# Sharing four score copies between ScalarE and VectorE, folding in one strided operation, and moving the first keys to another PSUM bank

## The chip, the cores and the metric

The kernel runs on one core of one Trainium2 chip. The metric is the device time of one execution in microseconds. It is a single launch, with all tensors in the chip's memory at the start and the output written there at the end.

## The reference

The input is x, 8 batches of 128 tokens with 512 channels, and a context of the same shape. Three blocks follow one another, each added to its input and followed by a layer norm:

```
x = layernorm(x + self_attention(x))      # 32 query heads, 8 key/value heads, 128 wide, 4-bit weights, causal mask
x = layernorm(x + cross_attention(x, ctx))
x = layernorm(x + expert_layer(x))        # dense product plus the two best of 8 low-rank experts
```

The change lies almost wholly in the second block, whose softmax runs over axis 0, which is the axis of batches and heads together:

```
Q, K, V = x @ Wq.T + bq, ctx @ Wk.T + bk, ctx @ Wv.T + bv       # 16 heads of 32 channels
Q, K, V = each as (8 batches * 16 heads) matrices of 128 tokens x 32
scores = einsum('bqd,bkd->bqk', Q, K) / sqrt(32)                  # b: 128 batch-head pairs
attn = softmax(scores, axis=0)                                    # over the 128 pairs, not over the keys
out = einsum('bqk,bkd->bqd', attn, V)
```

So for each query and each key position the largest of 128 scores, and the sum of 128 exponentials, are wanted: eight batches of sixteen heads.

## The kernel before

The program writes each engine's instruction stream by hand; engines meet only through semaphores, and each engine executes its own stream in order. PSUM has eight banks of 512 float32 columns, called banks[0] to banks[7].

**Self-attention** takes most of the time. It runs in phases; TensorE's `phase(f)` projects queries, keys and values for phase f + 1, computes scores and weighted values of phase f, and multiplies the finished heads of phase f - 1 with the output weights. The products rotate over banks 0, 1, 2 and 7 (`product_ps`). VectorE reads twelve of every sixteen output products out of PSUM (`add_out`, L1246); ScalarE reads the other four, those with u = 3, 7, 11, 15 (`scale_out`, L900), and GpSimd adds them (L711). `wait_out_read(eng, p, u)` waits until product u of part p has been read, on the semaphore of whichever engine reads it.

**The seam** between the blocks begins after the last `phase` call on TensorE (after the line `n = BPH * LAST` in TensorE's function). TensorE first waits for the keys' weights and the context, then for the read of output product 15 of part LAST - 2, and then computes the first four channels-by-token units of the cross-attention's keys (`keys(0..3)`, L1856, into `proj2_bank(i)`, banks[7]), interleaved with the last scores (L1622), transposes, weighted values and output products of self-attention. `out_bank` places the products of part LAST - 1 in banks 0, 1, 2 by u % 3. `turn_y` (L1810) transposes accumulated outputs back to token order, using banks 0, 1, 2 for the first four batches. The layer norm of the first four batches and the last sixteen output products (`outs_last`) follow, then the query units and the transposes of the other half.

**Cross-attention scores** are made a half at a time, four batches each: half 0 is batches 0 to 3, half 1 is batches 4 to 7. For one batch, `scores2(b)` (L1825) issues 16 matmuls into four whole banks, banks 0 to 3 for even b and 4 to 7 for odd b, so batch b needs batch b - 2 copied out. The matmuls go to 128 x 2048 results: 16 groups of 128 columns, a group being one head. `copy_scores2(b)` on ScalarE (L1069) moves all 2048 columns to the SBUF tile `xs[:, SLOT[b], :]` in one instruction and increments `scores2_copied`.

Around the scores, TensorE executes in this order: `scores2(0..3)`; a wait for three copies; eight units of 8 matmul instructions each for the other half's keys and queries (L1686); `scores2(4..7)`; a wait for seven copies; then `values(0..7)`, eight units for V (L1839, with a one-row matmul of the bias at L1835 ahead of the first three); and then `attend(b)` (L1941) and `turn_att(b)` (L1950) by batch.

VectorE computes, for each half h: `maximum2(h)`, three elementwise maxima over the four batches (L1431) and `fold`; `shift(h)`, subtracting the maximum from four batches (L1436), which releases ScalarE's exponentials (L1074) one by one; `add_exps(h)`, three elementwise sums (L1444) and `fold`. `fold` reduces 2048 columns, 16 groups of 128, to 128 columns in four halving operations (L1418 three times, L1419 once), each waiting for the one before through a semaphore. At the end of half 1 come the reciprocal and `weigh(b)` (L1463), one multiplication of 2048 columns for each batch, and `add_attended(b)` (L1469), which reads `turn_att`'s result.

After that follow the second layer norm, the expert layer and the output; the change does not touch them.

Of the kernel before, what the change touches and what calls it, by code (L numbers as in the profile page):

```python
# [14 lines left out]
AX = mybir.AxisListType  # L15

P = 128
NB = 8
T = NB * P
D = 512  # L20
KC = D // P
# [6 lines left out]
BPH = NB // 2  # L28
# [15 lines left out]
LN_GROUPS = [[(0, 2), (2, 2), (4, 2), (6, 2)], [(0, 2), (2, 2), (4, 2), (6, 2)], [(0, 2), (2, 2), (4, 2), (6, 1), (7, 1)]]  # L44
UNITS = 24
UNIT_ORDER = list(range(UNITS))
SLOT = [4, 5, 6, 7, 0, 1, 2, 3]
APART = 5
ROPE_TILES = [0, 2, 3, 4, 5]
# [4 lines left out]
OUTS = QPK * KC  # L54
RING = 3
LAST = 2 * NKV - 1
# [10 lines left out]
def wait(eng, sem, value):  # L67

    if isinstance(value, int) and value <= 0:
        return  # L70
    eng.wait_ge(sem, value)


def build(nc, t, out):
    with ExitStack() as ctx:
# [3 lines left out]
        def sem(name):  # L79
            return ctx.enter_context(nc.semaphore(name))  # L80
# [31 lines left out]
        def carve(*shape, base=None):  # L112
            n = int(np.prod(shape))
            if base is not None:
                at[0] = base
            a = at[0]
            at[0] += n
            assert at[0] <= ARENA, at[0]
            v = arena[:, a:a + n]
            if len(shape) == 2:  # L120
                return v.rearrange("p (a b) -> p a b", b=shape[1])
            if len(shape) == 3:
                return v.rearrange("p (a b c) -> p a b c", b=shape[1], c=shape[2])
            return v
# [93 lines left out]
        xs = carve(NB, XH * P, base=0)  # L218
# [68 lines left out]
        banks = [ps[:, i, :] for i in range(8)]  # L287
# [72 lines left out]
        proj2_copied = sem("proj2_copied")  # L360
        scored2 = sem("scored2")
        scores2_copied = sem("scores2_copied")
        shifted2 = sem("shifted2")
        apart2_ready = sem("apart2_ready")
        factor2_ready = sem("factor2_ready")
# [50 lines left out]
        def out_by_act(u):  # L416

            return u % KC == KC - 1

        def dve_index(u):  # L420
            return DVE_TILES * (u // KC) + u % KC

        def wait_out_read(eng, p, u):

            if out_by_act(u):
                wait(eng, out_scaled, KC * p + u // KC + 1)
            else:
                wait(eng, out_added, DVE_TILES * QPK * p + dve_index(u) + 1)
# [15 lines left out]
        def product_bank(name):  # L444
            return product_ps[PRODUCTS.index(name) % 4]
# [22 lines left out]
        def out_bank(p, u):  # L468

            if p == LAST - 1:  # L470
                return banks[u % 3]
            if p == LAST:
                return product_ps[u % 4]
            return product_bank(f"O{u}")
# [50 lines left out]

        def turn_y_bank(b):

            return banks[b % 3] if b < BPH else banks[5 + b % 2]

        def turn2_bank(layer, b):  # L530

# [4 lines left out]
        def proj2_bank(i):  # L536

            if i < KC:
                return banks[7]
            if i < 2 * KC:  # L540
                return banks[(3, 4, 0, 1)[i - KC]]
            return banks[i % 3]

        def scores2_banks(b):

            return ps[:, 4 * (b % 2):4 * (b % 2) + 4, :]
# [283 lines left out]
        def _(act):  # L830
# [79 lines left out]
            def copy_k2(i):  # L910

                n, half = i % KC, i // (2 * KC)
                act.wait_ge(proj2_done, UNIT_ORDER.index(i) + 1)
                nc.scalar.activation(k2_halves[half][:, n, :], proj2_bank(i), ACT.Identity,
# [145 lines left out]
            def copy_q2(i):  # L1060

                n, half = i % KC, i // (2 * KC + KC)
                act.wait_ge(proj2_done, UNIT_ORDER.index(i) + 1)
                nc.scalar.activation(q2_halves[half][:, n, :], proj2_bank(i), ACT.Identity,
                                     bias=bias_qk[:, n:n + 1]).then_inc(proj2_copied, 1)

            def copy_scores2(b):
                act.wait_ge(scored2, b + 1)
                nc.scalar.activation(xs[:, SLOT[b], :], scores2_banks(b).rearrange("p a n -> p (a n)"),  # L1069
                                     ACT.Copy).then_inc(scores2_copied, 1)  # L1070

            def exps2(b):
                act.wait_ge(shifted2, b + 1)
                nc.scalar.activation(xs[:, SLOT[b], :], xs[:, SLOT[b], :], ACT.Exp, scale=XSCALE).then_inc(exp2_done, 1)  # L1074

# [6 lines left out]
            def copy_v2(b):  # L1082

                i = 4 * KC + b
                act.wait_ge(proj2_done, UNIT_ORDER.index(i) + 1)
                nc.scalar.activation(v2[:, b, :], proj2_bank(i), ACT.Copy).then_inc(proj2_copied, 1)

            n = BPH * LAST
# [106 lines left out]
        def _(dve):  # L1195
# [174 lines left out]
            n = BPH * LAST  # L1370
# [31 lines left out]
            def step(ins):  # L1402

                nonlocal soft_steps
                soft_steps += 1
                ins.then_inc(soft_step, 1)
                dve.wait_ge(soft_step, soft_steps)
# [4 lines left out]
            def by_group(v):  # L1412
                return v.rearrange("p (g q) -> p g q", q=P)

            def fold(v, op, dst):

                for n in (1024, 512, 256):
                    step(nc.vector.tensor_tensor(v[:, 0:n], v[:, 0:n], v[:, n:2 * n], op))  # L1418
                step(nc.vector.tensor_tensor(dst, v[:, 0:P], v[:, P:2 * P], op))  # L1419

            def maximum2(h):

                for b in range(BPH * h + 1, BPH * (h + 1)):
                    maximum_with(h, b)
                fold(x_max, ALU.max, x_m[h])

            def maximum_with(h, b):

                first = BPH * h
                dve.wait_ge(scores2_copied, b + 1)  # L1430
                step(nc.vector.tensor_tensor(x_max, xs[:, SLOT[b], :], xs[:, SLOT[first], :] if b == first + 1 else x_max,  # L1431
                                             ALU.max))

            def shift(h, *tiles):
                for b in tiles or range(BPH * h, BPH * (h + 1)):
                    nc.vector.tensor_tensor(by_group(xs[:, SLOT[b], :]), by_group(xs[:, SLOT[b], :]), over_groups(x_m[h]),  # L1436
                                            ALU.subtract).then_inc(shifted2, 1)

            def add_exps(h):

                first = BPH * h
                for b in range(first + 1, first + BPH):
                    dve.wait_ge(exp2_done, b + 1)
                    step(nc.vector.tensor_tensor(x_sum, xs[:, SLOT[b], :], xs[:, SLOT[first], :] if b == first + 1 else x_sum,  # L1444
                                                 ALU.add))
# [16 lines left out]
            def weigh(b):  # L1462
                nc.vector.tensor_tensor(by_group(xs[:, SLOT[b], :]), by_group(xs[:, SLOT[b], :]), over_groups(x_r[b // BPH]),  # L1463
                                        ALU.mult).then_inc(weights2_ready, 1)
# [52 lines left out]
            for k in range(3):  # L1517
                products, tiles, count = first_products(k)
# [47 lines left out]
            for k in range(3):  # L1566
                products, tiles, count = first_products(k)
# [25 lines left out]
        def _(pe):  # L1593
# [68 lines left out]
            def project_out(p, u):  # L1662

                h, nt, half = u // KC, u % KC, p % 2
                if u == 0:
                    wait(pe, heads_ready, BPH * (p + 1))
                if nt == 0:
                    wait(pe, wo_ready, QPK * (p // 2) + h + 1)
                if p < LAST - 1:
                    wait_product_bank(p + 1, f"O{u}")  # L1670
                elif p == LAST - 1 and u >= 3:
                    wait_out_read(pe, p, u - 3)
                elif p == LAST:
                    wait(pe, proj2_copied, KC)
                    if u >= 4:
                        wait_out_read(pe, p, u - 4)
                for k, part in enumerate((heads_hi, heads_lo)):
                    mm = nc.tensor.matmul(out_bank(p, u), wo_sb[:, h, nt * P:(nt + 1) * P], part[:, half, h, :],  # L1678
                                          start=(k == 0), stop=(k == 1))
                mm.then_inc(out_done, 1)  # L1680
# [136 lines left out]

            def scores2(b):

                wait(pe, scores2_copied, b - 1)  # L1820
                half, tokens = b // BPH, slice((b % BPH) * P, (b % BPH + 1) * P)
                for n in range(KC):
                    for i in range(4):
                        rows = slice(XD * i, XD * i + XD)
                        mm = nc.tensor.matmul(scores2_banks(b)[:, i, n * P:(n + 1) * P], k2_halves[half][rows, n, tokens],  # L1825
                                              q2_halves[half][rows, n, tokens], start=True, stop=True)
                mm.then_inc(scored2, 1)
# [33 lines left out]
            n = BPH * LAST  # L1861
            pe.wait_ge(k2_in, 16)
            pe.wait_ge(ctx_in, 16 * 2 * KC)
            wait_out_read(pe, LAST - 2, OUTS - 1)
            keys(0, 0, 1, 2, 3)
            scores(n)
            scores(n + 1)
# [45 lines left out]
            pe.wait_ge(proj2_copied, 2 * KC)  # L1913
            for b in range(BPH):
                scores2(b)
            pe.wait_ge(scores2_copied, BPH - 1)
            for i in range(8, 12):
                wait(pe, proj2_copied, i - 2)
                channels_by_token(i, wk2, ctx_t[:, :, HALF:])
# [6 lines left out]
            pe.wait_ge(proj2_copied, 4 * KC)  # L1926
            for b in range(BPH):
                scores2(BPH + b)
            pe.wait_ge(scores2_copied, NB - 1)
            for b in range(NB):  # L1930
                values(b)

# [193 lines left out]
```

## Time and profile before

| what | value |
|---|---|
| median of 3 runs | 675.29 us (674.85 to 675.7) |
| the profiled execution's own time | 674.36 us |
| its span | 672.6 us |
| PE busy | 633.9 us, 94% |
| DVE busy | 547.4 us, 81% |
| ACT busy | 452.0 us, 67% |
| POOL busy | 407.0 us, 61% |
| granted TensorE clock, mean | 0.995 |

The span leaves 1.76 us of the profiled execution's time outside it. PE is TensorE's matmuls, PEld its weight loads, DVE is VectorE, ACT is ScalarE, POOL is GpSimd. A busy share is an average over stages that have different limits, so the stages are read one by one: the timeline gives the instructions of all engines in order of time with the idle time ahead of each and who ended it; the chain of waits follows the work that ended last backwards from the last instruction, and is shown in order of time; the windows view gives the busy time of each engine in a stretch and the granted clock.

### The profile page before, as it was taken

How to read it: one execution, taken by the hardware profiler on the slowest of the kernel's cores; microseconds unless marked ns; L12 is line 12 of the kernel's file. 1: busy time of each engine (PE TensorE's matmuls, PEld its weight loads, DVE VectorE, ACT ScalarE, POOL GpSimd, SP SyncE). 2: the span in 40 equal slices, each digit the busy share in tenths (PEclk: the TensorE clock that was granted, in tenths of full speed). 3: DMA queues.
4: the chain of work that ended last, by engine and by line, in shares of the span. 5: the costliest groups of instructions: out<-in, count | busy, mean ns of one | idle time of the engine just before them, and what ended most of it. 6: DMA issues, size and time to landing. Idle time of an engine off the chain costs nothing. (4 is left out here: it accounts for less than half of the span.)

```text
span 672.6 us, 11232 instructions
## 1 busy us (share of the span) xinstructions
PE 633.9 (94%) x3358; PEld 443.2 (66%) x3358; DVE 547.4 (81%) x944; ACT 452.0 (67%) x1293; POOL 407.0 (61%) x351
## 2 busy tenths in 40 slices
PE   8889999999999999999999999999998989978996
PEld 4557787777878778687777877856554444447552
DVE  5977898998989889899898998975462968998357
ACT  6598787969869788796976978776644545622100
POOL 1576899899799889989979888791240000012003
PEclk9999999999999999999999999999999998999998
DMA  7864532534442252153244223330010000020003
GB/s 237 260 167 117 165 94 67 164 86 108 120 132 48 79 164 56 36 165 83 64 116 121 57 55 104 106 105 18 0 64 1 0 1 1 0 98 2 1 0 125
DMA packets 30189, 57.00 MB, mean 85 GB/s; under 512 B 4784, under 2 KB 5040, under 8 KB 29616
## 3 DMA queue, kind: packets, MB, share of 16 engines
q1 hardware_dynamic: 30128, 56.28, 29.0%
q8 instruction: 27, 0.44, 0.3%
q14 instruction: 34, 0.28, 0.1%
HBM read 33.19 MB, written 2.10 MB: 52 GB/s over the span
## 5 line engine op out<-in xcount | busy, mean ns | idle before, releaser
L1216 DVE SCALAR_TENSOR_TENSOR arena<-ps,scales,arena 128x512 f32<-128x512 f32 x288 | 212.5, 745 | 27.2 <-PE ps L1604 11.2
L1604 PE MATMUL ps<-x_hi,w_sb 128*128 128x512 f32 x384 | 164.6, 429 | 8.3 <-DVE y L1246 3.4
L1246 DVE SCALAR_TENSOR_TENSOR y<-ps,out_scales,y 128x512 f32<-128x512 f32 x192 | 139.2, 744 | 16.9 <-PE ps L1678 16.6
L1604 PE MATMUL ps<-x_lo,w_sb 128*128 128x512 f32 x384 | 151.9, 396 | 0.0
L686 POOL TENSOR_TENSOR arena<-arena,consts 128x512 f32<-128x512 f32 x75 | 96.7, 1289 | 21.5 <-DVE arena L1216 20.4
L859 ACT ACTIVATE arena<-ps,small 128x128 f32<-128x128 f32 (+1 forms) x256 | 84.4, 360 | 36.6 <-DVE small L1224 31.2
L1678 PE MATMUL ps<-heads_hi,wo_sb 128*128 128x512 f32 x256 | 108.8, 425 | 0.1
L692 POOL TENSOR_TENSOR arena<-arena,consts 128x512 f32<-128x512 f32 x75 | 96.9, 1292 | 16.1 <-DMA arena<-arena 15.4
L711 POOL TENSOR_TENSOR y<-arena,y 128x512 f32<-128x512 f32 x64 | 82.5, 1289 | 32.5 <-ACT arena L900 30.5
L1604 PEld LDWEIGHTS ps<-x_hi,w_sb 128*128 128x128 f32 x384 | 72.8, 190 | 42.8 <-DVE arena L1216 10.7
L1678 PE MATMUL ps<-heads_lo,wo_sb 128*128 128x512 f32 x256 | 101.0, 394 | 0.0
L809 POOL TENSOR_SCALAR var_eps<-mean_var 128x2 f32<-128x2 f32 (+1 forms) x13 | 7.0, 542 | 154.7 <-DVE mean_var L1354 154.7
L702 POOL TENSOR_TENSOR arena<-arena 128x512 f32<-128x512 f32 x75 | 96.8, 1291 | 5.6
L850 ACT ACTIVATE arena<-ps,scales 128x512 f32<-128x512 f32 x96 | 67.3, 701 | 22.3 <-PE ps L1604 21.9
L1604 PEld LDWEIGHTS ps<-x_lo,w_sb 128*128 128x128 f32 x384 | 73.1, 190 | 10.2
L877 ACT ACTIVATE arena<-arena,small 128x128 f32<-128x128 f32 (+1 forms) x256 | 76.4, 400 | 0.0
L1622 PEld LDWEIGHTS ps<-arena 128*128 128x128 f32 x512 | 66.3, 191 | 8.0 <-issue 3.5
L1622 PE MATMUL ps<-arena 128*128 128x128 f32 (+1 forms) x512 | 64.3, 269 | 0.8 <-POOL arena L702 0.4
L1678 PEld LDWEIGHTS ps<-heads_hi,wo_sb 128*128 128x128 f32 x256 | 48.1, 188 | 20.9 <-issue 11.7
L859 ACT ACTIVATION_READ_ACCUMULATOR arena<-ps,small 128x1 f32 x256 | 58.0, 227 | 0.0
L900 ACT ACTIVATE arena<-ps,out_scales 128x512 f32<-128x512 f32 x64 | 44.7, 698 | 14.0 <-PE ps L1678 13.7
L1678 PEld LDWEIGHTS ps<-heads_lo,wo_sb 128*128 128x128 f32 x256 | 48.3, 189 | 7.1 <-issue 0.5
(153 smaller groups left out, 955.2 us busy)
## 6 DMA issues: line engine op xcount, KB each, us to landing
arena<-arena SPq DMA_DIRECT2D x160, 128.0 KB, 2.3
arena<-in_qkv SPq DMA_DIRECT2D x48, 256.0 KB, 3.9
arena<-in_o SPq DMA_DIRECT2D x32, 256.0 KB, 3.8
arena<-in_x_t SPq DMA_DIRECT2D x8, 256.0 KB, 3.8
y<-in_x SPq DMA_DIRECT2D x4, 512.0 KB, 4.3
arena<-in_ctx_t SPq DMA_DIRECT2D x8, 256.0 KB, 2.9
out<-y SPq DMA_DIRECT2D x8, 256.0 KB, 2.0
arena<-in_wk SPq DMA_DIRECT2D x1, 1024.0 KB, 5.0
```

The lines of the kernel that those rows point to most:

```text
L686: nc.gpsimd.tensor_tensor(by_pair(raw_cos[:, i % 2, :]), by_pair(raw[:, c % RING, :]), every_pair(cos_of(c)), ALU.mult).then_inc(cos_done, 1)
L692: nc.gpsimd.tensor_tensor(by_pair(turned[:, i % 2, :]), by_pair(turned[:, i % 2, :]), every_pair(sin_of(c)), ALU.mult).then_inc(sin_done, 1)
L702: nc.gpsimd.tensor_tensor(dst, by_block(raw_cos[:, i % 2, :]), by_block(turned[:, i % 2, :]), ALU.add).then_inc(rotated, 1)
L711: nc.gpsimd.tensor_tensor(dst, by_tile(out_part[:, k % 2, :]), dst, ALU.add).then_inc(part_added, 1)
L850: nc.scalar.activation(raw_of(p, c), group_bank(p, KC * c), ACT.Copy, scale=scale_of(p // 2, c, 0)).then_inc(act_scaled, 1)
L859: last = nc.scalar.activation(probs_part(n, i), score_ps[n % 2][:, score_part(i)], ACT.Exp, bias=neg_max[:, s, i:i + 1], accum_out=row_sum ...
L877: last = nc.scalar.activation(part, part, ACT.Copy, scale=row_inv[:, s, i:i + 1])
L1216: nc.vector.scalar_tensor_tensor(acc, group_bank(p, KC * c + g), scale_of(p // 2, c, g), acc, ALU.mult, ALU.add).then_inc(dve_scaled, 1)
L1246: nc.vector.scalar_tensor_tensor(dst, by_tile(out_bank(p, u)), out_scale_of(p // 2, u), dst, ALU.mult, ALU.add).then_inc(out_added, 1)
L1604: mm = nc.tensor.matmul(group_bank(p, u), w_sb[:, c, g, :], part[:, g, half * HALF:(half + 1) * HALF], start=(k == 0), stop=(k == 1))
L1622: mm = nc.tensor.matmul(bank[:, score_part(i)], queries, keys, start=False, stop=(n >= 2 or i == QPK - 1), skip_group_check=(n >= 2))
L1678: mm = nc.tensor.matmul(out_bank(p, u), wo_sb[:, h, nt * P:(nt + 1) * P], part[:, half, h, :], start=(k == 0), stop=(k == 1))
```

## The change

It has three parts. First, for batches 0, 1, 4 and 5 (the list `SHARED`) ScalarE copies the columns of the first two banks (0 to 1023) and VectorE copies those of the other two (1024 to 2047), with a second semaphore, `scores2_copied_too`; whoever waited for a copy now waits for both counts. VectorE issues its two copies of a half ahead of the maxima. Second, `fold` becomes one `tensor_reduce` over a view in which the 16 groups are the innermost axis, so it reads float32 values 128 elements apart. Third, the keys of half 0 (`keys(0..3)`) go to banks[0] in place of banks[7]; the output products of part LAST - 1 and the first four `turn_y` go to banks 1, 2, 7 in place of 0, 1, 2. With that the wait ahead of `keys(0)` is for output product 12 and not 15, and a wait for product 15 is added ahead of output product 2.

```diff
+SHARED = [0, 1, 4, 5]
@@ out_bank
             if p == LAST - 1:
-                return banks[u % 3]
+                return banks[(1, 2, 7)[u % 3]]
@@ turn_y_bank
-            return banks[b % 3] if b < BPH else banks[5 + b % 2]
+            return banks[(1, 2, 7)[b % 3]] if b < BPH else banks[5 + b % 2]
@@ proj2_bank
             if i < KC:
-                return banks[7]
+                return banks[0]
+        def wait_scores2_copied(eng, count):
+            wait(eng, scores2_copied, count)
+            wait(eng, scores2_copied_too, len([b for b in range(count) if b in SHARED]))
@@ ScalarE
             def copy_scores2(b):
                 act.wait_ge(scored2, b + 1)
-                nc.scalar.activation(xs[:, SLOT[b], :], scores2_banks(b).rearrange("p a n -> p (a n)"),
+                part = slice(0, 2 if b in SHARED else 4)
+                nc.scalar.activation(xs[:, SLOT[b], 0:512 * part.stop], scores2_banks(b)[:, part, :].rearrange("p a n -> p (a n)"),
                                      ACT.Copy).then_inc(scores2_copied, 1)
@@ VectorE
             def fold(v, op, dst):
-                for n in (1024, 512, 256):
-                    step(nc.vector.tensor_tensor(v[:, 0:n], v[:, 0:n], v[:, n:2 * n], op))
-                step(nc.vector.tensor_tensor(dst, v[:, 0:P], v[:, P:2 * P], op))
+                step(nc.vector.tensor_reduce(dst, v.rearrange("p (g q) -> p q g", q=P), AX.X, op))
+            def copy_half(b):
+                dve.wait_ge(scored2, b + 1)
+                nc.vector.tensor_copy(xs[:, SLOT[b], 1024:2048], scores2_banks(b)[:, 2:4, :].rearrange("p a n -> p (a n)")
+                                      ).then_inc(scores2_copied_too, 1)
             def maximum2(h):
+                for b in range(BPH * h, BPH * (h + 1)):
+                    if b in SHARED:
+                        copy_half(b)
@@ maximum_with
-                dve.wait_ge(scores2_copied, b + 1)
+                wait_scores2_copied(dve, b + 1)
@@ TensorE
+                elif p == LAST - 1 and u == 2:
+                    wait_out_read(pe, p - 1, OUTS - 1)
                 elif p == LAST:
-                    wait(pe, proj2_copied, KC)
+                    if u == 0:
+                        wait(pe, proj2_copied, KC)
@@ scores2
-                wait(pe, scores2_copied, b - 1)
+                wait_scores2_copied(pe, b - 1)
@@ seam
-            wait_out_read(pe, LAST - 2, OUTS - 1)
+            wait_out_read(pe, LAST - 2, OUTS - 4)
             keys(0, 0, 1, 2, 3)
@@ ahead of the units, and ahead of values
-            pe.wait_ge(scores2_copied, BPH - 1)
+            wait_scores2_copied(pe, BPH - 1)
-            pe.wait_ge(scores2_copied, NB - 1)
+            wait_scores2_copied(pe, NB - 1)
```

## Rows read from the trace of the kernel before

**Rows 1.** Page of the profile, busy time of the engines over the span

```profile
PE 633.9 (94%) x3358; PEld 443.2 (66%) x3358; DVE 547.4 (81%) x944; ACT 452.0 (67%) x1293; POOL 407.0 (61%) x351
```

**Rows 2.** Chain of waits, 440 to 560 us: start, duration (both us), what

```profile
450.66 3.67 PE ps L1856 x8
454.33 1.73 PE ps L1622 x16
...
523.26 27.75 PE ps L1686 x64
```

**Rows 3.** Timeline around the seam: start, us, engine, line, [idle before, releaser]

```profile
446.05 1.40 DVE L1246 SCALAR_TENSOR_TENSOR y<-ps,out_scales,y 128x512 f32<-128x512 f32 x2
...
449.85 0.67 ACT L900 ACTIVATE arena<-ps,out_scales 128x512 f32<-128x512 f32 x1
450.50 1.27 POOL L702 TENSOR_TENSOR arena<-arena 128x512 f32<-128x512 f32 x1
450.66 3.67 PE L1856 MATMUL ps<-arena 128*128 128x512 f32 x8 [1.45 <-ACT arena L900]
```

**Rows 4.** Timeline, score stage of half 0

```profile
517.79 7.18 ACT L1069 ACTIVATE arena<-ps 128x2048 f32<-128x2048 f32 x4 [1.29 <-PE ps L1825]
519.72 1.17 PE L1825 MATMUL ps<-w_area,arena 32*128 32x128 f32 x32 [1.10 <-ACT arena L1069]
```

**Rows 5.** Instructions grouped by line and shape: count, busy us, mean ns, idle before

```profile
L1069 ACT ACTIVATE arena<-ps 128x2048 f32<-128x2048 f32 x8 | 14.4, 1883 | 2.8 <-PE ps L1825 2.8
L1057 ACT ACTIVATE arena<-ps 128x512 f32<-128x512 f32 x4 | 2.2, 594 | 0.3 <-PE ps L1799 0.3
L1469 DVE TENSOR_TENSOR y<-ps,y 128x512 f32<-128x512 f32 x8 | 5.5, 686 | 0.2 <-PE ps L1950 0.2
L1418 DVE TENSOR_TENSOR late<-late 128x1024 f32<-128x1024 f32 x4 | 4.9, 1226 | 0.1
L1418 DVE TENSOR_TENSOR late<-late 128x512 f32<-128x512 f32 x4 | 2.8, 692 | 0.1
```

**Rows 6.** Timeline, end of half 0's sum and the score stage of half 1

```profile
549.46 0.29 DVE L1419 TENSOR_TENSOR late<-late 128x128 f32<-128x128 f32 x1
551.97 2.07 PE L1825 MATMUL ps<-arena,late 32*128 32x128 f32 x64 [0.98 <-ACT arena L1064]
553.20 7.19 ACT L1069 ACTIVATE arena<-ps 128x2048 f32<-128x2048 f32 x4 [1.48 <-PE ps L1825]
556.95 2.29 DVE L1431 TENSOR_TENSOR late<-arena 128x2048 f32<-128x2048 f32 x1 [7.20 <-ACT arena L1069]
```

**Rows 7.** Chain of waits, 530 us to the end: half 1 on VectorE

```profile
563.93 1.24 DVE late L1418
...
566.38 0.30 DVE late L1419
566.70 0.30 DVE late L1452
```

**Rows 8.** Instructions by line and shape: VectorE's reductions and a sum of equal size

```profile
L1525 DVE TENSOR_TENSOR late<-late 128x256 f32<-128x256 f32 x1 | 0.4, 426 | 0.0
L1523 DVE TENSOR_REDUCE late<-late 128x8 f32<-128x256 f32 x1 | 0.4, 420 | 0.0
```

**Rows 9.** Timeline, TensorE's values and the first attended batch

```profile
559.72 5.39 PE L1839 MATMUL ps<-arena 128*128 128x512 f32 x8
566.09 3.70 PE L1839 MATMUL ps<-arena 128*128 128x512 f32 x8
591.57 1.95 PE L1941 MATMUL ps<-arena 128*32 128x128 f32 x64
593.46 0.66 PE L1950 MATMUL ps<-consts,late 128*128 128x128 f32 x4
594.37 0.69 DVE L1469 TENSOR_TENSOR y<-ps,y 128x512 f32<-128x512 f32 x1
```

**Rows 10.** Windows: stretch, us, busy of five engines, granted clock, DMA

```profile
559.00:563.00 4.00, 4.00 (x6) 1.51 (x5) 3.93 (x3) 1.39 (x1) 0.00 (x0) 0.59 0.00 0
```

More of the change, by code:

```diff
@@ L362, in build @@
         scores2_copied = sem("scores2_copied")
+        scores2_copied_too = sem("scores2_copied_too")
         shifted2 = sem("shifted2")
```

## The prediction

> **What bounds the kernel now.** I read the page first, for the shares: TensorE is busy nearly throughout [rows 1]. That says little of a change inside one late stage, so the chain of waits came next, read from 440 us to the end, and then the timeline and the grouped instructions of the places where it changes engine. Three engines hold the end in turn. (a) At the seam TensorE stands idle for 1.45 us until ScalarE's L900 ends, then runs the keys and the scores, and the chain goes through it [rows 2, 3]. (b) In half 0 the score stage is an alternation of TensorE and ScalarE's four copies; when the third copy ends TensorE starts 27.75 us of units without a gap [rows 2, 4]. (c) In half 1 VectorE waits 7.20 us for the second copy [rows 6] and from there nearly everything to the second layer norm is VectorE's: maxima, fold, shift, sums, fold, weighing. TensorE's values run beside that and are almost as late: `attend(0)` starts at 591.57, straight behind them, and `turn_att(0)` ends at 594.12, while VectorE takes its result at 594.37 [rows 9]. So TensorE is only about 0.25 us ahead of the chain there. This is the number that decides how much of VectorE's gain arrives.
>
> **Part by part.** The sum is made against the profiled execution, 674.36 us (span 672.6 and 1.76 around it). It is 0.93 us under the median, and I take the difference off the median of 675.29.
>
> *The seam.* Before, `keys(0)` waits for product 15, read by ScalarE up to 450.52; now it waits for product 12, which is the second of the two VectorE instructions that end at 447.45 [rows 3]. Nothing else holds it: TensorE goes idle at 449.21 (450.66 less 1.45), so keys start there and gain 1.45 us. Next in TensorE's queue are the scores, which need GpSimd's last rotation, over at 451.77; they would start at 454.33 - 1.45 = 452.88, with 1.1 us to spare [rows 2, 3]. The wait for product 15, now ahead of output product 2, falls behind keys and two score sets and is long met (behind it on TensorE would stand the rest of the seam). The banks only change places in the same rotation of three, so no new wait arises there; moving `turn_y` costs nothing for the same reason. No DMA sits in this chain: bias and query weights are issued on their own conditions and are used much later. From the scores on, the seam is a chain of dependent short steps, so I let the whole 1.45 us through. Bounds: 0 and 1.45, plus 0.15 if the keys also pipeline into the product ahead of them.
>
> *The half copies.* ScalarE's copy costs 1883 ns for 2048 columns and 594 ns for 512 [rows 5], thus 0.84 ns a column, and 1.02 us for 1024. VectorE has no such copy in this trace. Its nearest rows are a tensor_tensor out of PSUM, 686 ns for 512 columns, equal to the 692 ns of the same from SBUF, and 1226 ns for 1024 columns in SBUF [rows 5], so 1.04 ns a column on a fixed 0.16 us: I take 1.23 us. Bounds: 0.7 us (half the time a column) and 1.9 us (ScalarE's whole copy, were the two engines to slow one another).
>
> *Half 0.* Before, from the first copy's start to TensorE's units: 523.26 - 517.79 = 5.47 us, three copies in line [rows 2, 4]. Now: VectorE's half 1.23 us, `scores2(2)` 1.2 us [rows 4], ScalarE's whole copy of batch 2 1.88 us [rows 5], and some 0.1 us of handovers: 4.4 us. Batch 1's halves end about when `scores2(2)` does and hold only batch 3, which the units don't wait for. Gain 1.05 us, and it is TensorE's, so it is passed on whole to 551. VectorE was idle when it takes the copies, so they delay nothing.
>
> *Half 1, VectorE.* Copies before: ready at 553.20, first maximum at 556.95, so 3.75 us [rows 6]. Now VectorE copies batch 4 and batch 5 one after the other, 2 x 1.23 + 0.04 = 2.50 us; the scores of batch 5 are there at 551.97 + 2.07 = 554.04, ahead of the second copy, and ScalarE's half ends about 555.2. Gain 1.25 us. Batch 6 then arrives at about 557.6, ahead of the second maximum, so no stall follows. *Fold.* Four steps and the gaps between them take from 563.93 to the next operation at 566.70, 2.77 us [rows 7]. One reduction has 2048 elements to read. At 256 elements a tensor_reduce costs 420 ns and a tensor_tensor 426 [rows 8], so at 2048 I take the latter's 2.29 us [rows 6], with a gap 2.31: gain 0.46 us each. The 8 results of that row cost nothing visible; the 128 here might add up to 0.1 us. What no row has is a long strided read out of SBUF. The nearest is L1469, which reads PSUM 32 floats apart and costs the 686 ns of a plain one [rows 5]: I take full rate, and as bounds 2.29 us and three times that for one fold. The two folds of half 0 end at 549.75 with the next score set not ready before 553.20 [rows 6]; they are hidden, with 3.45 us of cover (about as much after the change, since VectorE and TensorE both shift). VectorE's gain in half 1 is 1.25 + 0.92 = 2.17 us.
>
> *A rule that speaks against the fold.* The row above shows a stride costing nothing, but in PSUM. The Trainium skill ("SBUF — State Buffer", Specifications (TRN2)) says that SBUF is read in 16-byte lines, that full bandwidth needs two hits in a line, and that each crossing to a new line is penalised. Every element here is in another line. No run here shows the size of the penalty; by that rule the fold loses instead of gaining, which is the second rival below.
>
> *Half 1, TensorE.* `values` waits for the copy of batch 6, the third of four that take 7.19 us [rows 6], so 5.4 to 5.5 us from the first one's start, as in half 0; now 4.4: gain 1.05 us only. It then runs without a gap, ends 1.05 us earlier, and `turn_att(0)` ends at 593.07. VectorE, whose third weighing ended as L1469 began, is ready at 594.37 - 2.17 = 592.2 and waits some 0.9 us for it. `add_attended(0)` goes from 594.37 to about 593.1: 1.3 us come out of the 2.17, and the layer norm after it keeps this.
>
> Sum: 1.45 + 1.05 + 1.3 = 3.8 us. 675.29 - 3.8 = 671.5 us.
>
> **Rivals.** *No cold clock (faster still).* From 559 to 563 us the granted clock is 0.59, so TensorE is mostly at 1.2 instead of 2.4 GHz, just after the score stage with its narrow matmuls and waits; the first eight instructions of values take 5.39 us and eight warm ones 3.70 [rows 9, 10]. The fall is hidden behind VectorE today. The change shortens that sparse stretch by a microsecond in either half; in half 0, where one as sparse is followed at once by full matmuls, the clock doesn't fall. If it stays up, values end 1.05 + 1.69 us earlier and VectorE's 2.17 passes whole: 1.45 + 1.05 + 2.17 = 4.7, 670.6 us. For it: the shorter stretch. Against: the one trace that I have shows it fallen.
>
> *The strided fold at half rate (no change).* Each fold 0.16 + 2 x 2.13 = 4.43 us, 1.66 more than before. In half 1 VectorE then gains 1.25 and loses 3.3, so the chain from there is 2.1 us later; half 0's folds still end just under cover (3.3 of 3.45 us, plus 0.1 of difference in shifts). 1.45 + 1.05 - 2.1 = 0.4: 674.9 us. Against it: the strided PSUM row at full rate.
>
> *The fold at a third of the rate (slower).* 0.16 + 3 x 2.13 = 6.55 us, 3.8 more for each. Half 1: 7.6 - 1.25 = 6.3 later; half 0 overshoots its cover by about 4. Less the 2.5 of seam and half 0: some 8 us, 683 us. It decides from 4.65 us a fold, where the two of half 1 eat all gains: (1.45 + 1.05 + 1.25) / 2 = 1.88 above 2.77.
>
> *Copies that slow one another.* At 1.9 us for VectorE's 1024 columns, half 0 gains 0.4 us and VectorE's start in half 1 nothing; the folds' 0.9 is left there, and the total is 2.8: 672.5 us. *The seam's gain is lost* in its chain of handovers through five engines: 2.35, 672.9 us.
>
> **How the numbers follow.** Forecast as summed 0.38 (671.5); clock stays up 0.25 (670.6); copies slow one another 0.07; seam lost 0.08; fold at half rate 0.16 (674.9); fold at a third or worse 0.06. All but the last two are under 674.0, which is 0.2% below the median, about what a measurement of this kernel can tell from no change. So faster 0.78, same 0.16, slower 0.06. To leave out no more than 2 in 10 the range must reach the half-rate fold, up to 675.0, and down to 670.0 for the clock that stays up with 0.15 us of pipelining and the faster VectorE copy; the likeliest case's own range is 670.9 to 672.2.
>
> **What would show it.** Right: no idle time ahead of the first L1856 row, scores about 452.9; VectorE's copies 1.2 us each; TensorE's units at about 520.8 (523.26 less 1.45 and 1.05); folds as one TENSOR_REDUCE of 2.3 us; `attend(0)` right behind values and an idle stretch of some 0.9 us on VectorE ahead of the first L1469, with the clock still falling in values. If the clock doesn't fall there, that idle stretch is gone and the end comes 0.9 us earlier. Wrong: a TENSOR_REDUCE of 4.4 us or more, a VectorE copy near 1.9 us, or a new gap behind the scores of the seam.

## The result and the profile after

The changed kernel takes 673.77 us (median of 21 runs, 671.95 to 675.42) against 675.18 us of the kernel before in the runs taken with it (21 runs, 674.07 to 677.58). The ratio is 0.9971, with a 95% interval of 0.9962 to 0.998: faster, by 0.2 to 0.4%. The forecast was 3.8 us; 1.4 us of the medians came, and by the ratio 2.0. The profiled execution took 673.79 us, with a span of 671.9. The fold alone and the seam alone each had one slow run among eleven (793.79 and 792.01 us), which the figures given below leave out.

Single runs of either kernel lie up to 3.5 us apart, and most of that arises ahead of the seam, where all these kernels execute the same work. So I compare traces from a common point: the start of the last matmuls of weighted values ahead of the keys, L1658 before and L1673 after. It lies at 446.93 us before and 447.02 after, and between 445.9 and 449.9 in the traces below. Measured from it, the three traces of the changed kernel agree within 0.02 us at each mark and within 0.05 us at the end.

| us from that point | keys | units of half 0 | first maximum of half 1 | first weighing | first add of attended values | end of span |
|---|---|---|---|---|---|---|
| before | 3.73 | 76.33 | 110.02 | 140.83 | 147.44 | 225.67 |
| after | 2.13 | 73.66 | 106.24 | 138.90 | 146.46 | 224.88 |
| after - before | -1.60 | -2.67 | -3.78 | -1.93 | -0.98 | -0.79 |

The gain grows to 3.78 us by the first maximum of half 1, which is what the forecast wanted there. Then 1.85 us of it go between that maximum and the first weighing, and another 0.95 between the first weighing and the first add. These two losses are the subject of this study.

The seam and both score stages did as said. The first fence is the timeline of the changed kernel at the seam, to be read against [rows 3]: the keys follow the products with no idle time ahead of them, while ScalarE still reads product 15 (L907). The second is its chain of waits in half 0.

```profile
448.91 0.40 PE L1696 MATMUL ps<-heads_lo,wo_sb 128*128 128x512 f32 x1
449.15 3.60 PE L1874 MATMUL ps<-arena 128*128 128x512 f32 x8
449.94 0.67 ACT L907 ACTIVATE arena<-ps,out_scales 128x512 f32<-128x512 f32 x1
450.58 1.27 POOL L709 TENSOR_TENSOR arena<-arena 128x512 f32<-128x512 f32 x1
452.58 1.89 PE L1637 MATMUL ps<-arena 128*128 128x128 f32 x16
```

```profile
516.15 1.24 DVE arena L1430
...
517.52 1.21 PE ps L1843 x32
518.75 1.89 ACT arena L1077
520.68 27.75 PE ps L1704 x64
```

From the first copy to the units it is now 520.68 - 516.15 = 4.53 us, against 5.47 before [rows 2, 4]: a half copy on VectorE, one set of scores, one whole copy on ScalarE. The groups by line and shape of the changed kernel give the price of the new instructions: 1220 ns for the half copy, close to the 1.23 us taken, but 3661 ns for the fold that was put at 2.29 us.

```profile
L1425 DVE TENSOR_REDUCE late<-late 128x128 f32<-128x2048 f32 x4 | 14.6, 3661 | 0.1
L1430 DVE COPY arena<-ps 128x1024 f32<-128x1024 f32 x4 | 4.7, 1220 | 10.9 <-PE ps L1843 10.9
```

The next fence is the timeline of the changed kernel in half 1. The fold takes 560.24 to 563.93, 3.69 us with its gap where the four steps took 2.77 [rows 7]. Here the clock stays up in the values: the first eight instructions take 3.70 us, against 5.39 in [rows 9].

```profile
550.80 2.36 DVE L1430 COPY arena<-ps 128x1024 f32<-128x1024 f32 x2 [2.08 <-PE ps L1843]
553.26 2.29 DVE L1446 TENSOR_TENSOR late<-arena 128x2048 f32<-128x2048 f32 x1
556.38 3.70 PE L1857 MATMUL ps<-arena 128*128 128x512 f32 x8
560.24 3.66 DVE L1425 TENSOR_REDUCE late<-late 128x128 f32<-128x2048 f32 x1
563.93 0.29 DVE L1467 TENSOR_TENSOR late<-late 128x128 f32<-128x128 f32 x1
```

Then the attended batches, in the timeline and the windows of the changed kernel (us of the stretch, busy us of PE, PEld, DVE, ACT, POOL, the granted clock, DMA). TensorE waits 1.65 us ahead of `attend(0)` and 1.12 us ahead of `attend(1)`, and from 590 to 594 us the granted clock is 0.57, so TensorE is mostly at 1.2 GHz. `attend(1)` takes 1.93 us where the warm `attend(0)` takes 1.08, `turn_att(0)` 1.12 us where it took 0.66 in [rows 9], and VectorE stands idle for 0.87 us ahead of its first add.

```profile
588.26 1.08 PE L1959 MATMUL ps<-arena 128*32 128x128 f32 x32 [1.65 <-DVE arena L1478]
590.47 1.93 PE L1959 MATMUL ps<-arena 128*32 128x128 f32 x32 [1.12 <-DVE arena L1478]
592.33 1.12 PE L1968 MATMUL ps<-consts,late 128*128 128x128 f32 x4
593.48 0.69 DVE L1484 TENSOR_TENSOR y<-ps,y 128x512 f32<-128x512 f32 x1 [0.87 <-PE ps L1968]
```

```profile
588.00:590.00 2.00, 1.08 (x32) 0.81 (x32) 2.00 (x2) 0.59 (x1) 0.00 (x0) 1.00 0.74 311
590.00:594.00 4.00, 3.53 (x56) 2.71 (x60) 3.13 (x3) 0.60 (x2) 0.00 (x0) 0.57 0.57 225
594.00:600.00 6.00, 2.84 (x64) 1.97 (x52) 6.00 (x8) 1.19 (x2) 1.53 (x1) 1.00 0.00 0
600.00:604.00 4.00, 3.38 (x40) 2.91 (x40) 3.74 (x5) 0.96 (x2) 1.30 (x2) 0.57 0.00 0
```

### The profile page after: what moved, and what is told of

Read it like the earlier page. It is cut to its first block and busy times, and to the rows that moved or that the text cites. A ratio compares the mean times of both kernels' runs of the same rounds, so it can differ in the third digit from the quotient of the medians.

```text
span 671.9 us, 11223 instructions
## 1 busy us (share of the span) xinstructions
PE 634.8 (94%) x3358; PEld 445.2 (66%) x3358; DVE 556.1 (83%) x936; ACT 448.4 (67%) x1293; POOL 407.3 (61%) x351
## 5 line engine op out<-in xcount | busy, mean ns | idle before, releaser
L907 ACT ACTIVATE arena<-ps,out_scales 128x512 f32<-128x512 f32 x64 | 44.7, 699 | 13.9 <-PE ps L1696 13.6
```

## The experiments

The theory: (1) the seam and the copies each give what the trace shows, and add up; (2) the one-operation fold reads SBUF with a stride and pays for that; (3) the clock's fall at `attend(1)` costs the rest, and whether it falls there is a matter of the execution. The rivals: the parts depend on one another; the fold is slow for its 128 results, not its stride; the wait at the first add lies in the order of the steps; the fall at that place belongs to the changed kernel. The columns of the table at the end are those of the one above.

**The fold put back.**

```diff
-                step(nc.vector.tensor_reduce(dst, v.rearrange("p (g q) -> p q g", q=P), AX.X, op))
+                for n in (1024, 512, 256):
+                    step(nc.vector.tensor_tensor(v[:, 0:n], v[:, 0:n], v[:, n:2 * n], op))
+                step(nc.vector.tensor_tensor(dst, v[:, 0:P], v[:, P:2 * P], op))
```

> The changed kernel with the fold put back to its four halving steps. Theory A (the strided tensor_reduce, 3.66 us against 2.77 us for four steps and their gaps, is what ate the gain): VectorE's half 1 starts its maxima at 553.3 as in the changed kernel, but weighing starts near 584.1 us in place of 585.9, and the median falls 1 to 2 us below the changed kernel's, to a ratio of about 0.9945 against the kernel before. Rival B (TensorE or its clock holds the attended batches, so VectorE's time no longer counts): weighing starts earlier just the same, but the first add of attended values (593.48 us in the changed kernel) moves by less than 0.5 us, and the ratio stays near 0.997.

Measured: 671.21 us (5 runs), ratio 0.9937 (0.9923 to 0.9951). The first weighing comes at 137.03, 1.87 us earlier than in the changed kernel, the add at 143.73, 2.73 earlier. That is more than the folds' share: the clock does not fall in the attended batches here, it falls in the values again (window 555 to 560 us below), where it is almost hidden. Theory A, that the fold ate the gain, holds, and rival B falls. The timeline of this kernel shows how near it is: `attend(0)` begins at 587.73, right behind the values, `turn_att(0)` ends at 590.27 and VectorE's add starts at 590.30. This is the TensorE-bound meeting point that the prediction looked for, with nearly no wait.

```profile
583.60 6.69 DVE L1480 TENSOR_TENSOR arena<-arena,small 128x2048 f32<-128x2048 f32 x3
587.73 1.95 PE L1961 MATMUL ps<-arena 128*32 128x128 f32 x64
589.61 0.66 PE L1970 MATMUL ps<-consts,late 128*128 128x128 f32 x4
590.30 0.69 DVE L1486 TENSOR_TENSOR y<-ps,y 128x512 f32<-128x512 f32 x1
```

```profile
555.00:560.00 5.00, 5.00 (x8) 2.04 (x9) 4.90 (x4) 1.58 (x1) 0.00 (x0) 0.66 0.00 0
```

**The fold alone.** The kernel before with only the reverse of that diff.

> The kernel before with the one-operation fold alone. Theory A: each of the two folds of half 1 costs 0.92 us more than the four steps, so weighing begins 1.84 us later than the 587.76 us of before, and the whole is slower by 1.8 us, ratio 1.0027. Rival (the slow reduction is due to what runs beside it in the changed kernel): a tensor_reduce of 2.3 us, and a ratio under 1. The folds of half 0 should be hidden: TensorE's units are not delayed.

Measured: 677.68 us (10 runs), ratio 1.0037 (1.0023 to 1.0052). Four reductions of 3653 ns, units and first maximum where they were (76.34 and 110.03), first weighing 1.83 us later, end 2.04 later. So the fold is as slow without the other two parts, and half 0's folds are hidden, both as expected.

**The seam alone.** The kernel before with the bank choices and waits of the seam.

> The kernel before with only the bank of the first keys changed, and the waits that go with it. Theory: keys start 1.5 us earlier and the whole chain behind the seam keeps it, so the end is 1.5 us earlier, ratio 0.9978. Rival: the gain is partly absorbed behind the seam, or lost to a fall of TensorE's clock elsewhere; then the scores of half 0 start 1.6 us earlier but the end moves less than 1 us.

Measured: 673.91 us (10 runs), ratio 0.998 (0.9967 to 0.9992). Keys 1.60 us earlier, every later mark 1.72 to 1.74, and so the end. Nothing is absorbed.

**The copies alone.** The kernel before with `SHARED`, the half copies and their waits.

> The kernel before with the four shared copies alone: the keys' bank and the halving fold as before. Theory: units start 0.9 us earlier behind the scores of half 0, weighing 0.9 + 1.2 = 2.1 us earlier, and the end 1.8 to 2.1 us earlier (ratio 0.997), or 1.2 if the clock falls in the attended batches. Rival (a part of it needs the earlier seam): less than 1 us at the weighing.

Measured: 672.96 us (10 runs), ratio 0.9955 (0.994 to 0.9969). Units 0.92 us earlier, first maximum 2.02, first weighing and first add 2.03, end 1.86. The copies need nothing of the seam. At the first weighing seam and copies make 1.73 + 2.03 = 3.76 us, and the kernel with both (the halving one) shows 3.80.

**Four views of the same fold.** The changed kernel with a different view for each of the four folds, all over 2048 inputs; where each of the four views is used stands in the expectation. Three of them reduce other elements than the softmax needs, so this kernel serves to time the fold only; it ran once.

```diff
+                if form == "contiguous":
+                    step(nc.vector.tensor_reduce(dst, v.rearrange("p (q g) -> p q g", g=XH), AX.X, op))
+                elif form == "stride4":
+                    step(nc.vector.tensor_reduce(dst.rearrange("p (a s) -> p a s", s=4),
+                                                 v.rearrange("p (a g s) -> p a s g", g=XH, s=4), AX.X, op))
+                elif form == "few":
+                    step(nc.vector.tensor_reduce(dst[:, 0:XH], v.rearrange("p (g q) -> p q g", q=XH), AX.X, op))
```

> The changed kernel with a different view in each fold, all of 2048 float32 inputs: first contiguous groups of 16 (128 results), then groups of 16 read 4 floats apart (128 results), then groups of 128 read 16 floats apart (16 results) followed by the original one, last the original one, 16 read 128 floats apart. The sums and maxima it forms are of the wrong elements except in the original form. Theory of the stride: contiguous 2.3 us, 4 floats apart between 2.3 and 3.7, 16 floats apart 3.7, original 3.7. Rival, a cost for each of the 128 results (11 ns each): contiguous and 4 apart 3.7 us, 16 floats apart with few results 2.4 us, original 3.7.

VectorE's timeline of this kernel, in that order: contiguous 2.29 us, 4 floats apart 3.81, 16 apart with 16 results 3.60, 128 apart with 128 results 3.63 and 3.68. The number of results costs nothing; the stride does, and already at 16 bytes in full. The rival, a price for each result, falls.

```profile
525.07 2.29 DVE L1429 TENSOR_REDUCE late<-late 128x128 f32<-128x2048 f32 x1
543.17 3.81 DVE L1431 TENSOR_REDUCE late<-late 128x128 f32<-128x2048 f32 x1
559.72 3.60 DVE L1434 TENSOR_REDUCE late<-late 128x16 f32<-128x2048 f32 x1
563.35 3.63 DVE L1436 TENSOR_REDUCE late<-late 128x128 f32<-128x2048 f32 x1
583.66 3.68 DVE L1436 TENSOR_REDUCE late<-late 128x128 f32<-128x2048 f32 x1
```

**Writing apart instead of reading apart.** The last maximum or sum of each half writes its results with the groups innermost into the tile that is free at that time, and the fold reads them contiguously.

```diff
+                return spare.rearrange("p (q g) -> p g q", g=XH), by_group(xs[:, SLOT[b], :]), by_group(total)
...
+                step(nc.vector.tensor_reduce(dst, v.rearrange("p (q g) -> p q g", g=XH), AX.X, op))
```

> The changed kernel, but the last maximum and the last sum of each half write their 2048 results with the 16 groups innermost, 16 floats apart, and the fold is one tensor_reduce that reads contiguously. If writing apart costs nothing: folds 2.3 us, weighing 2.75 us earlier than in the changed kernel and 0.9 us earlier than with four halving steps. If writing apart costs what reading does (1.7 ns an element): the last step takes 3.7 us in place of 2.3, and weighing comes no earlier than in the changed kernel, within 0.3 us.

Measured: 673.81 us (12 runs), ratio 0.9974 (0.9959 to 0.9989), first weighing at 138.85, where the changed kernel has 138.90. The fold is down to 2.29 us and the two maxima ahead of it take 5.95 us, which took 4.62: the one that writes apart costs 1.3 us more. The gain of the one is the loss of the other; the stride costs on the write side as it does on the read side.

This kernel also bears on the clock. Its values run at a lowered clock for a while, `attend(0)` starts right behind them, and the clock stays up in the first attended batches: `attend(1)` takes 1.08 us, and the first add comes 6.61 us after the first weighing, against 7.56 in the changed kernel, whose first weighing comes within 0.05 us of this one. No matmul is added here.

```profile
556.07 5.95 DVE L1453 TENSOR_TENSOR late<-arena,late 128x2048 f32<-128x2048 f32 x2
562.06 2.29 DVE L1425 TENSOR_REDUCE late<-late 128x128 f32<-128x2048 f32 x1
590.91 1.08 PE L1965 MATMUL ps<-arena 128*32 128x128 f32 x32 [1.10 <-DVE arena L1484]
592.97 0.68 DVE L1490 TENSOR_TENSOR y<-ps,y 128x512 f32<-128x512 f32 x1
```

**The clock held up.** The changed kernel with matmuls that compute nothing used, where TensorE waits for weighings.

```diff
+            def keep_warm(count):
+                for _ in range(count):
+                    nc.tensor.matmul(banks[3][:, 0:7 * LOW], mask_b[:, 0:P], mask_b[:, :], start=True, stop=True)
+            keep_warm(6)
             attend(0)
+            keep_warm(4)
             attend(1)
```

(and 4 ahead of `attend(3)`, 8 ahead of `attend(4)`)

> The changed kernel with 22 small bf16 matmuls added on TensorE into a free bank where it only waits for VectorE's weighings: 6 ahead of attend(0), 4 ahead of attend(1), 4 ahead of attend(3), 8 ahead of attend(4). They compute nothing that is used. Theory A (the clock falls at attend(1) and turn_att(0) because TensorE waits there, and that costs 0.9 of the 1.9 us that weighing is early): no fall of the granted clock between 588 and 605, the first add of attended values comes some 0.9 us earlier after its weighing (7.56 us from the first weighing in the changed kernel, 6.6 with the clock up), and the end 0.8 us earlier than the changed kernel's. Rival B (the wait ahead of that add is due to the order of the steps, not to the clock): the clock stays up and the add stays where it was, within 0.3 us.

The first weighing stays at 138.89; the add comes at 145.51, 6.62 us after it in place of 7.56, and the end at 223.94 in place of 224.88. The window from 588 to 606 us shows a granted clock of 1.00, and `attend(1)` and `turn_att(0)` take 1.08 and 0.66 us. So the fall of the clock costs the changed kernel 0.94 us in the trace, as the kernel that writes apart says too (7.56 less 6.61). In the medians it does not show: 673.96 us (12 runs), ratio 0.9969 (0.9955 to 0.9982), against 0.9971; an interval of 0.27%, 1.8 us wide, can't tell 0.9 us, and this kernel's profiled execution reached the seam 2.8 us later than the changed kernel's.

```profile
591.10 1.08 PE L1959 MATMUL ps<-arena 128*32 128x128 f32 x32 [0.51 <-DVE arena L1478]
592.11 0.93 PE L1997 MATMUL ps<-mask_b 128*128 128x448 bf16 x4
593.30 1.08 PE L1959 MATMUL ps<-arena 128*32 128x128 f32 x32 [0.26 <-DVE arena L1478]
594.31 0.66 PE L1968 MATMUL ps<-consts,late 128*128 128x128 f32 x4
```

```profile
588.00:606.00 18.00, 14.64 (x212) 9.25 (x211) 17.66 (x17) 4.19 (x7) 2.84 (x2) 1.00 0.25 93
```

**The same on the halving fold.**

> The changed kernel with four halving steps in the fold and 16 such small matmuls, 4 each ahead of attend(1) and attend(3), 8 ahead of attend(4). Theory A: the halving kernel already runs the attended batches at full clock, so nothing is gained: the same ratio of 0.994 within 0.1%, though the clock's fall in the values may move. Rival B (waits of the order of steps): no change either; a slower time by over 0.5 us would say that the fillers delay the attended batches.

Measured: 671.55 us (6 runs), ratio 0.9938 (0.9917 to 0.9958), as expected, but in the trace the end is at 223.22, 1.09 us later than without the fillers. There `attend(0)` already comes late, behind values that run at a lowered clock, and the four fillers stand between it and `attend(1)`: VectorE waits 1.06 us for `turn_att(0)`. In these two kernels such work paid where TensorE had to wait anyway, and cost where it was itself late.

```profile
588.29 0.93 PE L1999 MATMUL ps<-mask_b 128*128 128x448 bf16 x4
589.15 1.08 PE L1961 MATMUL ps<-arena 128*32 128x128 f32 x32
590.86 0.69 DVE L1486 TENSOR_TENSOR y<-ps,y 128x512 f32<-128x512 f32 x1 [1.06 <-PE ps L1970]
```

**The changed kernel twice more**, unchanged.

> The changed kernel, unchanged, for a second profile. From the last weighted values of self-attention to the weighing nothing should move by over 0.1 us. Theory (where the clock falls is a matter of the execution): the first add of attended values comes either 6.6 us after the first weighing, with the clock up there, or 7.6 us, with the clock down, and nothing between. Rival (the fall at attend(1) belongs to the changed kernel): 7.6 us and a fall at the same place again.

> The same once more: 6.6 or 7.6 us from first weighing to first add by the theory, 7.6 us by the rival. The part of the kernel ahead of the seam should be what differs most between the three profiles.

Both show 7.57 us from first weighing to first add, and the clock down from about 589 to 593 us, with the common point at 445.91 and 446.86 us. As far as three profiles go, the rival holds: the place is the same in all, and the 6.6 us that my theory allowed never came. But the other kernels speak against a place fixed by TensorE's work: those with the halving fold, with the four views and with the writing apart issue the same up to the values, at the same marks within 0.05 us, and there the clock fell in the values. Their folds of half 0 on VectorE differ, and two traces with the same work up to there never differed: with the clock held up it stayed up in the values, as in the three of the changed kernel, and it fell in both kernels with the halving fold. Whether the clock falls in the values is thus no toss-up in these traces, but what decides it stays open.

For the fall at `attend(1)` the traces do show what goes ahead of it. In four, the three of the changed kernel and the one with four views, TensorE stands idle ahead of `attend(0)` for 1.65 us or more, and the clock falls at `attend(1)`. In the other eight it waits there 0.51 us or less, and the clock stays up at `attend(1)`, although three of them (the seam alone, the fold alone, writing apart) also wait 1.1 us ahead of `attend(1)`. The rows of the first repeat are those of the changed kernel, a microsecond earlier:

```profile
589.34 1.93 PE L1959 MATMUL ps<-arena 128*32 128x128 f32 x32 [1.12 <-DVE arena L1478]
591.21 1.12 PE L1968 MATMUL ps<-consts,late 128*128 128x128 f32 x4
```

All kernels from the common point (us):

| kernel | keys | units | first maximum of half 1 | first weighing | first add | end of span |
|---|---|---|---|---|---|---|
| before | 3.73 | 76.33 | 110.02 | 140.83 | 147.44 | 225.67 |
| seam alone | 2.13 | 74.60 | 108.30 | 139.10 | 145.71 | 223.93 |
| copies alone | 3.73 | 75.41 | 108.00 | 138.80 | 145.41 | 223.81 |
| fold alone | 3.73 | 76.34 | 110.03 | 142.66 | 149.27 | 227.71 |
| after | 2.13 | 73.66 | 106.24 | 138.90 | 146.46 | 224.88 |
| after, clock held up | 2.11 | 73.66 | 106.24 | 138.89 | 145.51 | 223.94 |
| after, writing apart | 2.13 | 73.66 | 106.24 | 138.85 | 145.46 | 223.89 |
| after, halving fold | 2.12 | 73.64 | 106.22 | 137.03 | 143.73 | 222.13 |
| the same with fillers | 2.12 | 73.64 | 106.22 | 137.03 | 144.78 | 223.22 |

## Why the prediction was right and where it failed

The sign and the range held: 673.77 us lies between 670.0 and 675.0. But it lies outside the likeliest case's own range, 670.9 to 672.2; the whole range holds it only because it was stretched to reach the fold at half rate. The forecast itself, 671.5, was 2.3 us too fast, and its 3.8 us were about twice what came. That the median still fell below 674.0, the line that the prediction drew for faster, is in part luck: the trace keeps only 0.8 us, which would have made 674.5.

*The seam*, 1.45 us: right, and a little small. The keys begin 1.60 us earlier and 1.74 arrive at the end. The 0.15 us of pipelining that I kept as a bound is real, and another 0.13 appears between the keys and the scores of half 0: 0.08 of it up to the scores behind the keys, which take 3.60 us for 3.67, and the rest after them.

*The half copies*: right in each term. VectorE's copy 1.22 us for 1.23 assumed; half 0 gained 0.94 us by the chain and 0.92 with the copies alone, for 1.05 (the handovers were put too low); and in half 1 the two copies take 2.46 us up to the first maximum where it was 3.75, a gain of 1.29 for 1.25. Only 1.11 of it arrives, because TensorE's scores begin 1.09 us after the units in place of 0.98, and VectorE's copy 0.07 us later after them than ScalarE's did before; the same 0.18 is missing with the copies alone. The rival of engines that slow one another is out: ScalarE's two copies of 1024 columns, which run beside VectorE's, take 1.94 us together, for 1.02 each assumed:

```profile
516.15 1.94 ACT L1077 ACTIVATE arena<-ps 128x1024 f32<-128x1024 f32 x2 [1.29 <-PE ps L1843]
516.15 2.36 DVE L1430 COPY arena<-ps 128x1024 f32<-128x1024 f32 x2 [8.81 <-PE ps L1843]
```

*The fold*, a gain of 0.46 us each: wrong in sign. This is the step that failed. I took full rate from a strided read of PSUM and set aside a rule about SBUF that said otherwise. Each fold of half 1 costs 3.69 us in place of 2.77, a loss of 0.92. The right answer was the rule's, with a smaller penalty than the half-rate rival gave it: 3.66 us instead of 4.43. With the measured loss of 0.92 in place of 1.66 for each fold, that rival's sum is 1.45 + 1.05 + 1.25 - 1.84 = 1.9 us, and the trace shows 1.93 at the first weighing. The error cost the forecast less than 2 x 1.38 us, because the sum had let only 1.3 of VectorE's 2.17 us through: with no gain and no loss from the fold, its terms would have given 1.45 + 1.05 + 1.25 = 3.75.

*The clock*: the likeliest case had it fall in the values once more, so that TensorE would arrive 0.9 us behind VectorE; the rival had it stay up, so that all of VectorE's gain would pass. It did stay up in the values, but it fell at `attend(1)`. There the values, done 5 us earlier than before, leave TensorE waiting for VectorE's weighings, and the cost of 0.94 us is about what the likeliest case charged for another reason; that the two agree is chance. The idle stretch of VectorE ahead of its first add (0.87 us) was thus foretold in place and size with the wrong cause, and "the clock stays up in the values" did not bring the 0.9 us that I had written for it. I had looked for what is late next if TensorE becomes the bound, and not for what an idle TensorE costs. The wait ahead of `attend(0)` is itself the slow fold's doing, by an estimate: `attend(0)` starts 2.34 us after the first weighing (588.26 - 585.92), which with the halving fold would be 137.03 + 2.34 = 139.37 us from the common point, and the values end at 139.59 even with their clock up. So the 0.94 us may be a second price of the fold; no run has the halving fold with the clock up in the values.

The account in the trace: 3.78 us gained at the first maximum, less 2 x 0.92 for the folds, less 0.95 for the clock, less 0.19 in the tail, is 0.8 us. The tail's loss lies in the last layer norm, where a GpSimd step on the chain takes 0.43 us that took 0.19 before; it takes 0.19 with the seam alone too and 0.43 with the copies alone and the fold alone, and why is open:

```profile
668.69 0.19 POOL L809 TENSOR_SCALAR var_eps<-mean_var 128x1 f32<-128x1 f32 x1 [1.37 <-DVE mean_var L1354]
667.79 0.43 POOL L816 TENSOR_SCALAR var_eps<-mean_var 128x1 f32<-128x1 f32 x1 [1.36 <-DVE mean_var L1362]
```

The first row is of the timeline before, the second of the changed kernel's.

The medians show 1.4 us and the ratio's interval 1.4 to 2.6, so the trace undershoots it. The rest may lie in executions in which the clock stays up in the attended batches, or in the part ahead of the seam, which differs between executions by more; no run here assigns it. Without the fold the change would have been worth 3.54 us in the trace and 0.6% in the ratio, which is close to the forecast; that version, 671.21 us, beats both kernels.

## What to carry to other kernels

A fused instruction is cheaper than its steps only if its view reads at the same rate: price a strided view by a row of the same memory, and where there is none, let the range and the likeliest value follow the slower bound. Halving with contiguous operands (2.77 us for 2048 columns) beat one strided reduction (3.69). When an engine is freed to run ahead of another, look at what it does while it waits: a TensorE that waits may come back at half its clock, and the critical engine then pays.

## What the runs showed of the hardware

VectorE's tensor_reduce over 2048 float32 from SBUF took 2.29 us with contiguous reads, the same as an elementwise operation of that size, and 3.60 to 3.81 us with reads 16, 64 or 512 bytes apart, thus 1.7 to 1.8 ns an element instead of 1.04; the number of results (16 or 128) made no difference. An elementwise operation that wrote its results 64 bytes apart in SBUF cost 5.95 - 2.29 = 3.66 us with the gap ahead of it, the same. Out of PSUM, reads 128 bytes apart cost nothing extra: 686 ns for 512 elements, where contiguous SBUF operands took 692 [rows 5]. The Trainium skill ("SBUF — State Buffer", Specifications (TRN2)) tells of 16-byte lines with a penalty for each crossing; the four views agree in kind, since 16 bytes already cost all of it, and give the size, 0.57 to 0.66 of the contiguous time on top. Reads 8 bytes apart were not tried.

The granted clock fell for some 3.4 us at a time, in three places of the late part: in the values (before, the fold alone, both kernels with the halving fold, the four views, writing apart), in the attended batches 0 and 1 (the changed kernel three times, the four views), and some ten microseconds later (these, the fold alone, the seam alone, writing apart). With the copies alone and with the clock held up it fell nowhere from 540 us until TensorE had finished; once TensorE has finished, it falls in every trace. It cost 0.94 us in the second place. In the first it cost 0.09 us at most (6.70 us from weighing to add with the halving fold, against 6.61), because there VectorE is behind. In the third it cost nothing: from the first add to the end the changed kernel takes 78.42 us with the fall and 78.43 with the clock held up.
